# First expert layer of a two-layer decoder: expert tiles taken in pairs, the two 48-channel tails in different partition halves

## Chip, cores and metric

The program runs on one core of a Trainium2 chip. The metric is the device time of one execution in microseconds (us). Its engines are named as in the profile: PE is TensorE (PEld its weight loads, PEldq its instruction queue), DVE is VectorE, ACT is ScalarE, POOL is GpSimd, SP is SyncE, which here issues transfers (SPq).

## What is computed

A decoder of two layers over 32 sequences of 64 tokens, 256 channels, all in float32. Each layer has a self attention, a cross attention and a mixture of experts, each followed by a layer norm. The change lies in the first mixture of experts: 2048 tokens, 16 experts of 176 inner channels, the best 4 for each token, and a shared part.

```python
scores = jax.nn.softmax(xt @ Wg.T, axis=-1)
...
topi = jax.lax.top_k(masked, TOPK)[1]
weights = jnp.take_along_axis(scores, topi, axis=1) * ROUTE_SCALE
combine = jnp.zeros((T, E), xt.dtype).at[jnp.arange(T)[:, None], topi].add(weights)
h = jax.nn.silu(jnp.einsum('td,eid->eti', xt, W1)) * jnp.einsum('td,eid->eti', xt, W3)
expert_out = jnp.einsum('eti,edi->etd', h, W2)
y = jnp.einsum('etd,te->td', expert_out, combine)
z = jax.nn.silu(xt @ Ws1.T) * (xt @ Ws3.T) @ Ws2.T
```

## The kernel before

Everything stands in one program; the stages follow each other in blocks, and all engines meet at a barrier at the end of a block. The block `moe0` (from L1278) is the first mixture of experts. Tokens are copied by GpSimd into `xs`, a table in memory sorted by expert, of 79 tiles (`NT`) of 128 rows, each tile of one expert. Then each engine runs its own loop over the 79 tiles, four tiles to a turn of the loop (`tile_pipeline`, L1189), with the last seven written out; waits on semaphores couple the loops. For one tile the steps are:

- SyncE (`load`) reads the tile's place from a table and fetches its 128 rows of 256 channels into one of four buffers `XG`.
- TensorE (`rows`, L1590) turns them with two transposes; ScalarE (`rows`, L1455) copies them to `XGT`.
- TensorE (`gate_up`, L1598) multiplies with the expert's `W13`: 352 columns, 176 for the gate and 176 for up, over two halves of the 256 channels. A float32 product is two passes in the trace, so these are four instructions.
- ScalarE (`silu`, L1459) takes the silu of the gate, VectorE (`product`, L1534) multiplies it with up into `H` (128 tokens x 176 channels).
- TensorE (`turn_product`, L1604 and L1605) turns `H` in two pieces, 128 channels and the tail of 48; ScalarE copies both into `HT` (L1463, L1464). Rows 48 to 127 of the tail piece are zero, set once by GpSimd.
- TensorE multiplies with `W2A` (L1618, the first 128 inner channels) and `W2B` (L1620, the tail; its rows 48 to 127 are zeros, loaded by SyncE), 256 columns each.
- VectorE (`step`, L1542) copies the result to `Y`, ScalarE (`store`) issues its transfer to `ys`.

The register with the expert's number is loaded by `expert(j)` (L1585) before gate and up and again before W2A.

Two more things run beside it. GpSimd, when it has scattered the tokens, gathers the results of the first 12 token tiles (`EARLY`) from `ys`, four rows of results for each token, and adds them to `X` (`fetch_row` L1212, `add_rows`). After the tenth of these (`t == 9`) it computes a root for the next layer norm (`root_on_pool`, L1269 and L1270). VectorE leaves its loop twice for that norm: at tile 56 for the moments, at tile 68 for the normalization, which waits for the root:

```python
if t == 9:
    fx.l1.root_on_pool(nc, pool, fx.neghalf, own)
...
tile_pipeline(dve, step, NT, ((56, lambda: fx.l1.moments_on_dve(nc, dve, fx.X, r.steps)),
                              (68, lambda: fx.l1.apply_on_dve(nc, dve, fx.X))))
```

At the end TensorE has five filling products (`busy`, L132), and then comes the barrier.

## Time and profile before

| | us |
|---|---|
| median of three runs | 1228.31 |
| lowest and highest | 1223.89, 1232.03 |
| profiled execution, its time | 1227.53 |
| profiled execution, its span | 1225.5 |
| loop of the first experts on TensorE | 424.2 to 622.5 |
| barrier behind it | 627.2 |

The span runs from the first to the last instruction of the program; the time has 2.0 us more around it. In a line of the timeline the columns are the start, the duration, engine, line, operation, what is written and read, and how many instructions in a row; in square brackets is how long the engine was idle before and what ended it. The busy time of a product on PE contains its way through the array, so two products that follow each other without a gap overlap in the timeline: what one costs is the distance of two starts.

### The profile page before, as it was taken

To read this page: it belongs to the slowest core of one execution; us is meant where nothing else is said; L and a number is where in the kernel's file an instruction comes from. 1 tells how busy PE (TensorE), PEld (TensorE's weight loads), DVE (VectorE), ACT (ScalarE), POOL (GpSimd) and SP (SyncE) were. 2 spreads that over 40 slices of the span, in tenths; PEclk is the share of its full clock that TensorE was granted. 3 is DMA by queue.
4 is the path that set the end of the run, shared out by engine and by line. 5 is a ranking of instruction groups with operands and counts; after the bars stand their busy time and mean duration, and the time that the engine had idled before them with its cause. 6 is when DMAs were issued, how large, how long until landed. Compare 5 with 4: busy or idle time off the path is not lost. (4 is left out here: it accounts for less than half of the span.)

```text
span 1225.5 us, 29187 instructions
## 1 busy us (share of the span) xinstructions
PE 1107.1 (90%) x10342; PEld 871.7 (71%) x10343; DVE 474.1 (39%) x1234; ACT 500.3 (41%) x1301; POOL 443.6 (36%) x565
## 2 busy tenths in 40 slices
PE   5889888999989899999987999988649999999997
PEld 2567676776645577777766778776528989999997
DVE  1226465455557133323335666664383000000422
ACT  0424544344443233333335566664403434333342
POOL 2022012131124886787735664223034200200433
PEclk8999999999999999999989999999878999999999
DMA  6039918202137365565453110000056655655672
GB/s 196 18 93 356 352 36 301 96 24 75 53 138 231 121 197 176 159 195 148 136 215 154 42 50 19 20 20 2 5 177 224 206 168 175 205 172 173 202 242 83
DMA packets 116521, 173.18 MB, mean 141 GB/s; under 512 B 17440, under 2 KB 94096, under 8 KB 114960
## 3 DMA queue, kind: packets, MB, share of 16 engines
q1 hardware_dynamic: 89936, 128.46, 32.1%
q0 software_dynamic: 9696, 26.75, 6.7%
q10 hardware_dynamic: 16784, 16.49, 4.1%
q8 instruction: 76, 1.25, 0.4%
q14 instruction: 29, 0.24, 0.1%
HBM read 105.07 MB, written 65.27 MB: 139 GB/s over the span
## 5 line engine op out<-in xcount | busy, mean ns | idle before, releaser
L2589 PE MATMUL bank<-m_XGT,m_w 128*128 128x128 f32 x1248 | 149.4, 279 | 0.0
L2589 PEld LDWEIGHTS bank<-m_XGT,m_w 128*128 128x128 f32 x1248 | 146.4, 196 | 0.5 <-issue 0.5
L2603 PE MATMUL bank<-w,m_HT 128*128 x624 | 141.0, 379 | 0.0
L2603 PEld LDWEIGHTS bank<-w,m_HT 128*128 128x128 f32 x624 | 115.8, 190 | 14.0
L2421 ACT ACTIVATE m_HT<-bank,m_b 128x128 f32<-128x128 f32 x312 | 88.8, 368 | 81.9 <-PE bank L2589 78.5
L1598 PE MATMUL bank<-m_W,m_XGT 128*128 x316 | 107.1, 462 | 0.6 <-ACT m_XGT L1455 0.5
L2381 POOL DMA_INDIRECT m_GA<-ys,r_pos x32 | 32.1, 1005 | 130.0 <-SPq L2336 121.3
L1455 ACT ACTIVATE m_XGT<-bank 128x256 f32<-128x256 f32 x79 | 30.3, 383 | 119.8 <-DVE m_US L1542 117.6
L1212 POOL DMA_INDIRECT GA<-ys,r_pos x64 | 64.3, 1005 | 31.4 <-issue 22.7
L381 POOL TENSOR_SCALAR l_rs<-l_mv 128x2 f32<-128x2 f32 x16 | 3.6, 225 | 194.2 <-DVE l_mv L622 194.0
L1392 POOL DMA_INDIRECT xs<-X,r_pos x64 | 63.4, 990 | 27.1 <-issue 13.7
L1534 DVE TENSOR_TENSOR m_H<-bank,m_SG 128x176 f32<-128x176 f32 x79 | 27.0, 341 | 117.1 <-ACT m_SG L1459 117.1
L1598 PEld LDWEIGHTS bank<-m_W,m_XGT 128*128 128x128 f32 x316 | 54.0, 191 | 18.4 <-issue 1.5
L2367 POOL DMA_INDIRECT xs<-X,r_pos x32 | 32.0, 1000 | 61.1 <-DMA xs<-X,r_pos 35.2
L2432 ACT ACTIVATE m_Y<-bank 128x256 f32<-128x256 f32 x39 | 15.0, 383 | 92.4 <-PE bank L2603 92.4
L1618 PE MATMUL bank<-m_W2A,inputs 128*128 x158 | 47.6, 384 | 1.6 <-ACT inputs L1464 0.9
L1831 ACT ACTIVATE l_WX<-bank 128x512 f32<-128x512 f32 x64 | 33.8, 603 | 35.1 <-PE bank L2086 35.1
L1620 PE MATMUL bank<-m_W2B,inputs 128*128 x158 | 47.0, 379 | 0.0
L1542 DVE COPY m_US<-bank 128x256 f32<-128x256 f32 x79 | 33.5, 425 | 34.3 <-PE bank L1620 31.6
L59 PE MATMUL bank<-XT,inputs 128*128 128x512 f32 x96 | 43.1, 595 | 1.5 <-ACT raw L451 0.8
L2505 DVE TENSOR_TENSOR X<-bank,X 128x512 f32<-128x512 f32 x8 | 5.5, 692 | 89.8 <-PE bank L2565 89.8
L498 ACT ACTIVATE l_W<-l_W 128x512 f32<-128x512 f32 x32 | 19.4, 630 | 48.7 <-DVE l_W L648 48.7
(369 smaller groups left out, 2311.6 us busy)
## 6 DMA issues: line engine op xcount, KB each, us to landing
m_w<-in_m_w SPq DMA_DIRECT2D x35, 1024.0 KB, 5.2
xs<-zeros SPq DMA_DIRECT2D x1, 10112.0 KB, 33.7
ys<-zeros SPq DMA_DIRECT2D x1, 10112.0 KB, 36.0
ys<-m_US ACTq DMA_DIRECT2D x79, 128.0 KB
m_GS<-xs SPq DMA_DIRECT2D x72, 128.0 KB, 2.2
w<-in_m_w SPq DMA_DIRECT2D x8, 1024.0 KB, 14.9
m_W<-in_w SPq DMA_DIRECT2D x2, 2816.0 KB, 13.6
xs<-zeros SPq DMA_DIRECT2D x1, 4992.0 KB, 19.1
```

The source lines that it names most:

```text
L59: last = nc.tensor.matmul(dst, stills[i], movings[i], start=i == 0, stop=i == n - 1)
L1212: pool.indirect_dma_start(out=fx.GA[:, t % 2 * (t < EARLY), k, :], out_offset=None, in_=fx.ys, in_offset=bass.IndirectOffsetOnAxis(ap=fx.p ...
L1392: pool.indirect_dma_start(out=fx.xs, out_offset=bass.IndirectOffsetOnAxis(ap=r.pos[:, t, k:k + 1], axis=0), in_=fx.X[:, t, :], in_offset=N ...
L1542: nc.vector.tensor_copy(Y[:, b % 2, :], BY[b % 2][:, 0:DIM]).then_inc(y_used, 1)
L1598: last = nc.tensor.matmul(BU[b % 2][:, 0:IW], XGT[:, b % 2, m * P:(m + 1) * P], W13[:, m, bass.ds(e, 1), :], start=m == 0, stop=m == KC - 1)
L1618: nc.tensor.matmul(BY[b % 2][:, 0:DIM], HT[:, b % 2, 0, :], W2A[:, bass.ds(e, 1), :], start=True, stop=False)
L1620: nc.tensor.matmul(BY[b % 2][:, 0:DIM], HT[:, b % 2, 1, :], W2B[:, bass.ds(e, 1), :], start=False, stop=True).then_inc(y_full, 1)
L1831: nc.scalar.activation(WX[:, t, r].rearrange("p m c q -> p (m c q)"), SB[r][:], ACT.Exp, scale=D32 ** -0.5).then_inc(x_used.sem, 1)
L2381: pool.indirect_dma_start(out=GA[:, t, k, :], out_offset=None, in_=fx.ys1, in_offset=bass.IndirectOffsetOnAxis(ap=fx.pos1[:, t, k:k + 1], ...
L2421: last = nc.scalar.activation(HT[:, b % 2, at, :], BU[i][:, c * P:(c + 1) * P], ACT.Gelu, bias=b1[:, b % WB, at:at + 1])
L2589: last = nc.tensor.matmul(BU[i][:, c * P:(c + 1) * P], w1[:, b, m, lo:lo + P], XGT[:, b % 2, m * P:(m + 1) * P], start=m == 0, stop=m == K ...
L2603: last = nc.tensor.matmul(BY[b % 2][:, 0:DIM], HT[:, b % 2, c, :], w2[:, bass.ds(e, 1), c, :], start=c == 0, stop=c == CH - 1)
```

## The change

The loops take two tiles at a time (`pair_pipeline`). For a pair j, j+1:

- VectorE writes the first 128 channels of each product to its own buffer of `H`, and the two tails of 48 side by side into a third, at columns 0 and 64. Three transposes in place of four turn them; the tails then lie in partitions 0 to 47 and 64 to 111 of one piece. ScalarE copies all three with one instruction.
- The tail of tile j is multiplied with `W2B` over 48 rows. The tail of tile j+1 needs its weights in partitions 64 to 111, so SyncE loads them for each pair into a small buffer `odd` (48 x 256), two buffers in turn, and TensorE waits for `ld_odd`. The zeros of `W2B` are no longer loaded, and GpSimd clears a quarter of what it cleared.
- TensorE keeps the expert's number in a register from gate and up to W2A where both lie in the same turn of the loop: six loads for four tiles in place of eight.
- The order of the steps changes on each engine. TensorE goes gate and up of both next tiles, rows of the two after, W2A twice, the tails, and the turn of the next pair.

```diff
+def pair_pipeline(engine, step, n, visits=(), done=0):
+
+    for at, visit in (*visits, (n - PEEL, None)):
+        with engine.Fori(done // 4, at // 4) as i:
+            for b in range(0, 4, 2):
+                step(i * 4 + b, b, None)
+        if visit:
+            visit()
+        done = at
+    for j in range(n - PEEL, n, 2):
+        step(j, j % 4, n - 1 - j)
...
-        W2A, W2B = sb("W2A", [P, E0, DIM]), sb("W2B", [P, E0, DIM])
+        W2A, W2B, odd = sb("W2A", [P, E0, DIM]), sb("W2B", [P, E0, DIM]), sb("odd", [P, 2, DIM])
-        SG, H, HT = sb("SG", [P, 2, I0]), sb("H", [P, 2, I0]), fx.HT
+        SG, H, HT = sb("SG", [P, 2, I0]), sb("H", [P, 3, P]), fx.HT
...
-                sp.dma_start(W2B[KI:P], fx.zeros[KI:P].unsqueeze(1).broadcast_to([P - KI, E0, DIM])).then_inc(ld_w, 16)
                 sp.wait_ge(r.placed, 2)
 
+                def load_odd(e, b):
+                    sp.dma_start(odd[HALF:HALF + KI, b // 2].unsqueeze(1),
+                                 io["w2"][P:I0, bass.ds(e, 1), :]).then_inc(ld_odd[b // 2], 16)
+
+                def expert(j):
+                    return sp.value_load(r.texp[0:1, bass.ds(j, 1)], min_val=0, max_val=E0 - 1)
+
                 def load(j, b, checked=None):
+                    if b % 2:
+                        e = expert(j - BEHIND)
                     if checked is not None:
                         need = sp.value_load(r.tneed[0:1, bass.ds(checked, 1)], min_val=1, max_val=TILES)
                     s = sp.value_load(r.tslot[0:1, bass.ds(j, 1)], min_val=0, max_val=NT - 1)
                     sp.wait_ge(t_full, j + 1)
+                    if b % 2:
+                        load_odd(e, (b - BEHIND) % 4)
...
+                for j in range(NT - BEHIND, NT - 1, 2):
+                    e = expert(j)
+                    sp.wait_ge(y_full, j - 3)
+                    load_odd(e, j % 4)
...
-                def turned_product(j, b):
-                    act.wait_ge(ht_full, j + 1)
-                    nc.scalar.activation(HT[:, b % 2, 0, :], BH[b % 2][:, 0:P], ACT.Copy)
-                    nc.scalar.activation(HT[0:KI, b % 2, 1, :], BH[b % 2][0:KI, P:2 * P], ACT.Copy).then_inc(ht_used, 1)
+                def turned_pair(j):
+                    act.wait_ge(ht_full, j + 2)
+                    nc.scalar.activation(HT[:, 0:3, :].rearrange("p c t -> p (c t)"), BH[0][:, 0:3 * P],
+                                         ACT.Copy).then_inc(ht_used, 2)
 
                 def store(j, b):
                     s = act.value_load(r.tslot[0:1, bass.ds(j, 1)], min_val=0, max_val=NT - 1)
@@ -1469,13 +1497,18 @@
                     act.dma_start(rows_out[:, bass.ds(s, 1), :], Y[:, b % 2, :].unsqueeze(1)).then_inc(stored[b % 2], 16)
 
                 def step(j, b, ahead):
-                    if follows(ahead, 3):
-                        rows(j + 3, b + 3)
                     if follows(ahead, 2):
                         silu(j + 2, b + 2)
-                    if follows(ahead, 1):
-                        turned_product(j + 1, b + 1)
-                    store(j, b)
+                    if follows(ahead, 3):
+                        silu(j + 3, b + 3)
+                    for k in (4, 5):
+                        if follows(ahead, k):
+                            rows(j + k, b + k)
+                    if follows(ahead, 2):
+                        turned_pair(j + 2)
+                    for k in range(2):
+                        if follows(ahead, k):
+                            store(j + k, b + k)
...
                 silu(0, 0)
                 shared_rows(PAIRS - 1)
+                silu(1, 1)
                 rows(2, 2)
                 load(6, 2)
-                silu(1, 1)
-                turned_product(0, 0)
-                tile_pipeline(act, step, NT)
+                rows(3, 3)
+                turned_pair(0)
+                pair_pipeline(act, step, NT)
...
                 def product(j, b):
                     dve.wait_ge(gate, j + 1)
-                    nc.vector.tensor_tensor(H[:, b % 2, :], BU[b % 2][:, I0:IW], SG[:, b % 2, :],
+                    at = HALF * (b % 2)
+                    nc.vector.tensor_tensor(H[:, b % 2, :], BU[b % 2][:, I0:I0 + P], SG[:, b % 2, 0:P], ALU.mult)
+                    nc.vector.tensor_tensor(H[:, 2, at:at + KI], BU[b % 2][:, I0 + P:IW], SG[:, b % 2, P:I0],
                                             ALU.mult).then_inc(h_done, 1)
 
-                def step(j, b, ahead):
-                    if follows(ahead, 2):
-                        product(j + 2, b + 2)
+                def result(j, b):
                     dve.wait_ge(y_full, j + 1)
                     dve.wait_ge(stored[b % 2], 8 * (j + (2 - b % 2)))
                     nc.vector.tensor_copy(Y[:, b % 2, :], BY[b % 2][:, 0:DIM]).then_inc(y_used, 1)
 
+                def step(j, b, ahead):
+                    for k in (2, 3):
+                        if follows(ahead, k):
+                            product(j + k, b + k)
+                    for k in range(2):
+                        if follows(ahead, k):
+                            result(j + k, b + k)
+
+                dve.wait_ge(padded, 2)
                 product(0, 0)
                 product(1, 1)
-                tile_pipeline(dve, step, NT, ((56, lambda: fx.l1.moments_on_dve(nc, dve, fx.X, r.steps)),
+                pair_pipeline(dve, step, NT, ((56, lambda: fx.l1.moments_on_dve(nc, dve, fx.X, r.steps)),
                                               (68, lambda: fx.l1.apply_on_dve(nc, dve, fx.X))))
...
                 def gate_up(j, b):
-                    e = expert(j)
+                    e = kept[b % 4] = expert(j)
                     pe.wait_ge(t_used, j + 1)
                     for m in range(KC):
                         last = nc.tensor.matmul(BU[b % 2][:, 0:IW], XGT[:, b % 2, m * P:(m + 1) * P],
                                                 W13[:, m, bass.ds(e, 1), :], start=m == 0, stop=m == KC - 1)
                     last.then_inc(u_full, 1)
 
-                def turn_product(j, b):
-                    pe.wait_ge(h_done, j + 1)
-                    nc.tensor.transpose(BH[b % 2][:, 0:P], H[:, b % 2, 0:P], fx.ident[:])
-                    nc.tensor.transpose(BH[b % 2][0:KI, P:2 * P], H[:, b % 2, P:I0], fx.ident[:]).then_inc(ht_full, 1)
-
-                def step(j, b, ahead):
+                def turn_pair(j, ahead):
+                    pe.wait_ge(h_done, j + (2 if follows(ahead, 3) else 1))
+                    nc.tensor.transpose(BH[0][:, 0:P], H[:, 0, :], fx.ident[:])
                     if follows(ahead, 3):
-                        rows(j + 3, (b + 3) % 4)
+                        nc.tensor.transpose(BH[0][:, P:2 * P], H[:, 1, :], fx.ident[:])
+                    nc.tensor.transpose(BH[0][:, 2 * P:3 * P], H[:, 2, :], fx.ident[:]).then_inc(ht_full, 2)
+
+                def down_pair(j, b, both, first, e):
+                    if not first:
+                        pe.wait_ge(y_used, j)
+                    pe.wait_ge(ht_used, j + 2)
+                    if both:
+                        pe.wait_ge(ld_odd[b // 2], 4 * (j - b) + 16)
+                    for k in range(len(e)):
+                        nc.tensor.matmul(BY[k][:, 0:DIM], HT[:, k, :], W2A[:, bass.ds(e[k], 1), :],
+                                         start=True, stop=False)
+                    nc.tensor.matmul(BY[0][:, 0:DIM], HT[0:KI, 2, :], W2B[0:KI, bass.ds(e[0], 1), :],
+                                     start=False, stop=True).then_inc(y_full, 1)
+                    if both:
+                        nc.tensor.matmul(BY[1][:, 0:DIM], HT[HALF:HALF + KI, 2, :], odd[HALF:HALF + KI, b // 2, :],
+                                         start=False, stop=True).then_inc(y_full, 1)
+
+                kept = [None] * 4
+
+                def step(j, b, ahead, first=False):
+                    e = [kept[b], kept[b + 1]] if b % 4 == 2 else [None, None]
+                    for k in (2, 3):
+                        if follows(ahead, k):
+                            gate_up(j + k, b + k)
+                    both = follows(ahead, 1)
+                    for k in range(2):
+                        if e[k] is None and (k == 0 or both):
+                            e[k] = expert(j + k)
+                        if follows(ahead, k + 4):
+                            rows(j + k + 4, (b + k) % 4)
+                    down_pair(j, b, both, first, e[0:2 if both else 1])
                     if follows(ahead, 2):
-                        gate_up(j + 2, b + 2)
-                    if follows(ahead, 1):
-                        turn_product(j + 1, b + 1)
-                    e = expert(j)
-                    if not follows(ahead, 2):
-                        pe.wait_ge(y_used, j - 1)
-                    pe.wait_ge(ht_used, j + 1)
-                    nc.tensor.matmul(BY[b % 2][:, 0:DIM], HT[:, b % 2, 0, :], W2A[:, bass.ds(e, 1), :],
-                                     start=True, stop=False)
-                    nc.tensor.matmul(BY[b % 2][:, 0:DIM], HT[:, b % 2, 1, :], W2B[:, bass.ds(e, 1), :],
-                                     start=False, stop=True).then_inc(y_full, 1)
+                        turn_pair(j + 2, ahead)
 
                 pe.wait_ge(sh_used, 2 * SC * GROUPS)
                 rows(0, 0)
                 rows(1, 1)
                 shared_down(GROUPS - 1, (0,))
                 pe.wait_ge(r.placed, 3)
-                pe.wait_ge(ld_w, 80)
+                pe.wait_ge(ld_w, 64)
                 gate_up(0, 0)
                 shared_down(GROUPS - 1, (1,))
+                gate_up(1, 1)
                 rows(2, 2)
-                gate_up(1, 1)
-                turn_product(0, 0)
+                rows(3, 3)
+                turn_pair(0, None)
                 pe.wait_ge(z_used, PAIRS)
-                tile_pipeline(pe, step, NT)
+                step(0, 0, None, True)
+                step(2, 2, None)
+                pair_pipeline(pe, step, NT, done=4)
```

On TensorE, inside the loop, for one tile before. L1590 are rows, L1598 gate and up, L1604 and L1605 the turn, L1618 W2A, L1620 W2B:

```order
L1590 MATMUL bank<-ident,m_GS 128x128 x2
L1585 ISA
L1585 TENSOR_LOAD r_table
L1585 ISA x2
L1596 REGISTER_ALU
L1598 ISA
L1598 MATMUL bank<-m_W,m_XGT 128x352
L1598 ISA
L1598 MATMUL bank<-m_W,m_XGT 128x352
L1604 MATMUL bank<-ident,m_H 128x128
L1605 MATMUL bank<-ident,m_H 48x128
```

and the second half of a pair's steps in the changed kernel, the same engine and place, without register loads between (L1641 gate and up, L1633 rows, L1659 W2A, L1661 and L1664 the tails, L1647 to L1650 the turn):

```order
L1641 MATMUL bank<-m_W,m_XGT 128x352
L1641 ISA
L1641 MATMUL bank<-m_W,m_XGT 128x352
L1633 MATMUL bank<-ident,m_GS 128x128 x4
L1659 ISA
L1659 MATMUL bank<-m_W2A,inputs 128x256
L1659 ISA
L1659 MATMUL bank<-m_W2A,inputs 128x256
L1661 REGISTER_ALU
L1661 MATMUL bank<-m_W2B,inputs 128x256
L1664 MATMUL bank<-m_odd,inputs 128x256
L1647 MATMUL bank<-ident,m_H 128x128
```

The turn stood directly behind the next tile's gate and up, one tile behind its own; now it stands behind the tails and follows its own pair's gate and up by rows, W2A and tails.

On VectorE, at the end of the loop that leads to tile 68, before:

```order
L1534 TENSOR_TENSOR m_H<-bank,m_SG 128x176
L1542 COPY m_US<-bank 128x256
L1192 REGISTER_ALU
L1192 COMPARE_AND_BRANCH
L1275 TENSOR_SCALAR X<-X,l_mv,l_rs 128x256 x4
```

and in the changed kernel:

```order
L1569 TENSOR_TENSOR m_H<-bank,m_SG 128x128
L1570 TENSOR_TENSOR m_H<-bank,m_SG 128x48
L1575 REGISTER_ALU
L1576 COPY m_US<-bank 128x256 x2
L1205 REGISTER_ALU
L1205 COMPARE_AND_BRANCH
L1288 TENSOR_SCALAR X<-X,l_mv,l_rs 128x256 x4
```

The products and the copies now come in twos; the normalization (four instructions behind the wait for the root) stands where it stood, after the copy of tile 67.

## Rows read from the trace of the kernel before

**Rows 1.** The page's table of engines: busy us, share of the span.

```profile
PE 1107.1 (90%) x10342; PEld 871.7 (71%) x10343; DVE 474.1 (39%) x1234; ACT 500.3 (41%) x1301; POOL 443.6 (36%) x565
```

**Rows 2.** Timeline of TensorE, one tile of the first experts and the next.

```profile
500.77 0.38 PE L1590 MATMUL bank<-ident,m_GS 128*128 128x128 f32 x2
500.99 1.35 PE L1598 MATMUL bank<-m_W,m_XGT 128*128 x4
502.18 0.27 PE L1604 MATMUL bank<-ident,m_H 128*128 128x128 f32 x1
502.29 0.27 PE L1605 MATMUL bank<-ident,m_H 128*48 128x128 f32 x1
502.40 0.60 PE L1618 MATMUL bank<-m_W2A,inputs 128*128 x2
502.83 0.60 PE L1620 MATMUL bank<-m_W2B,inputs 128*128 x2
503.26 0.38 PE L1590 MATMUL bank<-ident,m_GS 128*128 128x128 f32 x2
```

**Rows 3.** Timeline of all engines around VectorE's visit at tile 68.

```profile
596.41 0.42 DVE L1542 COPY m_US<-bank 128x256 f32<-128x256 f32 x1 [0.39 <-PE bank L1620]
...
597.63 1.04 POOL L1270 TENSOR_TENSOR l_rs<-l_rs,neghalf 128x4 f32<-128x4 f32 x1
...
598.71 1.38 DVE L1275 TENSOR_SCALAR X<-X,l_mv,l_rs 128x256 f32<-128x256 f32 x4 [1.87 <-POOL l_rs L1270]
...
600.39 0.33 PE L1604 MATMUL bank<-ident,m_H 128*128 128x128 f32 x1
```

**Rows 4.** Timeline of GpSimd, the first fetch of two neighbouring token tiles.

```profile
576.60 1.03 POOL L1212 DMA_INDIRECT GA<-ys,r_pos  x1 [1.37 <-issue]
...
587.59 1.03 POOL L1212 DMA_INDIRECT GA<-ys,r_pos  x1 [1.37 <-DVE m_US L1542]
```

**Rows 5.** Timeline of the end of the block, all engines.

```profile
615.43 0.72 POOL L1232 TENSOR_TENSOR X<-X,GA 128x256 f32<-128x256 f32 x1
...
622.07 0.59 PE L1620 MATMUL bank<-m_W2B,inputs 128*128 x2
...
622.50 4.46 PE L132 MATMUL bank<-ones 128*128 128x512 f32 x10
...
627.22 1.91 POOL L1765 MEMSET l_VS<- 128x2176 f32 x1 [11.07 <-POOLq L1318]
```

**Rows 6.** Timelines of TensorE and its weight loads around column halves.

```profile
167.41 0.63 PE L810 MATMUL bank<-ident,X 128*128 128x128 f32 x4 [0.39 <-DVE l_V L579]
167.97 2.12 PE L855 MATMUL bank<-l_V,l_W 128*64 128x68 f32 x64
170.01 0.70 PE L59 MATMUL bank<-inputs,l_xwk 128*128 128x512 f32 x1
...
170.55 0.19 PEld L59 LDWEIGHTS bank<-inputs,l_xwk 128*128 128x128 f32 x1 [0.24 <-issue]
170.98 0.19 PEld L59 LDWEIGHTS bank<-inputs,l_xwk 128*128 128x128 f32 x1 [0.24 <-issue]
```

**Rows 7.** Timeline of TensorE at the loop's start.

```profile
424.19 0.38 PE L1590 MATMUL bank<-ident,m_GS 128*128 128x128 f32 x2
```

**Rows 8.** Timeline from gate and up to the product, ScalarE and VectorE.

```profile
504.88 0.31 ACT L1459 ACTIVATE m_SG<-bank 128x176 f32<-128x176 f32 x1
...
505.22 0.34 DVE L1534 TENSOR_TENSOR m_H<-bank,m_SG 128x176 f32<-128x176 f32 x1 [1.24 <-ACT m_SG L1459]
```

**Rows 9.** Line L1585, 500 to 600 us: ns min, median, max of the loads.

```profile
L1585 PEldq TENSOR_LOAD <-r_table x78: 295/302/628, 500.6 to 597.5; - x78
```

**Rows 10.** Waits of SyncE, 500 to 630 us: total, times, longest.

```profile
SPq L1338 <- PE bank L1590: 45.7, 37, 2.5
```

**Rows 11.** The page's DMA issues: KB each, median us to landing.

```profile
m_W2B<-zeros SPq DMA_DIRECT2D x1, 1280.0 KB, 33.2
```

**Rows 12.** Windows of 4 us: busy per engine, then PEclk, DMA share, GB/s.

```profile
630.00:634.00 4.00, 2.81 (x8) 2.25 (x8) 0.00 (x0) 1.15 (x2) 2.10 (x5) 0.50 0.98 337
```

10 lines of the change are left out of this document (5 added, 5 removed).

## The prediction, made before the changed kernel ran

> **What bounds the kernel now.** The page's table of engines comes first: TensorE is busy 90% of the span, no other engine over 41% [rows 1]. That is an average over six stages, so the next view is the stretch that the change touches: the timeline of the first expert layer. One tile there is six steps on TensorE, and their starts are the whole period: the two transposes of rows take 0.22 us (500.77 to 500.99), gate and up 1.19, the two transposes of H 0.11 each, W2A 0.43, W2B 0.43, and the next tile starts at 503.26, 2.49 after this one [rows 2]. No step waits. So a tile costs what TensorE issues, and two tiles 4.98 us.
>
> But the layer ends where three engines meet, and there a second view matters: who waits for whom at the visit that VectorE makes at tile 68 (apply_on_dve). Its copy of tile 67 starts at 596.41, then it sits idle for 1.87 us until GpSimd's power instruction (start 597.63, in root_on_pool) is done, and starts the four normalizations at 598.71; TensorE's next transpose of H is at 600.39, some 0.3 us late [rows 3]. GpSimd is not waiting for the experts at that time: it fetches and adds one token tile per 10.99 us (576.60, 587.59, with gaps for which the profile names its own issue or the usual 1.37 us) [rows 4]. The root hangs behind the tenth of these. So **the tenth token tile on GpSimd, at 598.7 us, is a fixed date**, and TensorE now arrives at it almost exactly on time. After it come tiles 68 to 78 on TensorE; the last W2B starts at 622.07, the five filling matmuls at 622.50, and all engines pass the barrier at 627.2 [rows 5].
>
> **The change part by part, on TensorE, per two tiles.** Removed: one of four transposes of H, 0.11 us. Kept: four row transposes (0.44), two times gate and up (2.38), three transposes (0.33), two W2A (0.86), together 4.01 us, from [rows 2]. What is left is the price of the two tails, 0.86 us today as two W2B products over 128 rows. They now use 48 rows each, one from partition 0 and one from partition 64, so they are matmuls of the 64-row form. Fewer rows shorten nothing by themselves: a start-to-start step goes with the columns that stream (0.22 for 256 per pass, 0.11 for 128). What could shorten is the pair running side by side. The trace has no two row halves with 128 columns, but it has column halves: 64 passes of 68 columns take 2.04 us (167.97 to 170.01) [rows 6]. A pass of 128 columns steps by 0.11, so 64 of 68 columns one after another would be some 3.7; two at a time did run. The bounds for the tails are then 0.43 us (fully side by side), 0.64 (each product has two passes, and if they are issued product by product only the middle two overlap) and 0.86 (no overlap). I take 0.43, which the column halves are nearest to.
>
> The same rows price what is added: entering and leaving that form. Four transposes starting at 167.41 should occupy 4 x 0.11 plus a cold first step of 0.03; the next form starts after 0.56, so 0.09 is lost. In the 2.04 us, 32 steps of 68/128 x 0.107 make 1.82, so 0.22 is lost inside and at the exit, of which I put half on the exit. The first full-width pass then takes 0.54 us to the second (170.01 to 170.55), where later ones step by 0.43 (170.55 to 170.98): another 0.11, because its weights were not loaded ahead [rows 6]. Entering costs the same exposed weight load, some 0.1. Together 0.09 + 0.1 + 0.09 + 0.1 = **0.38 us for each visit**, one visit per pair; ends 0.25 and 0.55. The pair is then 4.01 + 0.43 + 0.38 = 4.82 us against 4.98: 0.16 saved per pair, 6 us over 39.5 pairs, if nothing else held the layer.
>
> What the row shows is a loss at each boundary. The Trainium skill says the same in "TensorEngine Tiling (Array Packing)", Tiling Modes, Key Properties: changing the tiling mode drains TensorE. It speaks against this change, and the trace agrees with it. The same page's Theoretical Speedup table offers up to twice the rate for a dimension of 64 or less; taken alone that would make the pair 4.44 us and 21 us in all, and the boundary losses above take 15 of them away.
>
> **The latency of the pair.** The turn of H now waits for the product of a tile whose gate and up ended only 0.44 + 0.86 + 0.43 + 0.2 = 1.9 us before. The chain is: silu starts 0.2 us after the last gate pass has been followed (504.67, a pitch after 502.18, to 504.88), lasts 0.31, the product starts at 505.22 and lasts 0.34 [rows 8]; split in two instructions it is some 0.47. That is 1.1 us, under 1.9, so the wait is covered by rows, W2A and tails; were that cover gone it would cost 0.2 to 1.1 us per pair. Queued behind this wait on TensorE is the next gate and up with its register load.
>
> **Registers.** A load of an expert number takes TensorE's sequencer 0.30 us [rows 9] and stands beside running matmuls now, since [rows 2] has no gap. Two of eight per four tiles go. Value: 0. **ScalarE** makes one copy of 384 columns instead of two copies: off the path, 0. **SyncE**: one more register load and one more 48 KB transfer per pair. It now waits 45.7 us for TensorE in 37 loads from 500 on, 1.24 us of 2.49 [rows 10], so a load costs it 1.25 and the pair 2.5 plus some 1.25 for the new one, 3.75 of 4.82: still ahead. The new transfer is asked for after the rows of tile j+5 and needed 5.7 us later; at the one place where SyncE issues the next layer's weights it may come up to 4 us late, once, before tile 68. **W2B's zeros** (1,280 KB, landed 33.2 us after issue at 358) [rows 11] are gone, but their cover was 25 us: 0. In the **start**, the loop begins with rows at 424.19 [rows 7]; gate and up of tile 1 now stands directly before its own turn, so some 1 us is lost there.
>
> **The sum.** Result of tile 67: 425.2 + 34 x 4.82 = 589.1, plus the 3.1 us of small stalls that lie between 424.19 and 596.41 today (172.2 us for 68 x 2.486 = 169.1): 592.2. VectorE then waits 6 us for the root at 598.7, not 1.9. Nothing of what was won before that date is left. TensorE can still do the next 4.8 us of work (to 597) and then stands idle until the products of tiles 70 and 71 are there: 598.7 + 1.3 for the normalizations + 0.9 for four product instructions, so 601.0. From there: turn 0.33, pairs 70 and 72 9.64, pair 74 with one set of rows 4.60, pair 76 with one gate and up 1.19 + 0.86 + 0.81 + 0.22 = 3.08, and the last single tile with an exposed copy 1.8. End at 620.4, against 622.5. An idle stretch has its price too: after 2.4 us idle at 627 the granted clock of 630 to 634 is 0.50, the 1.2 GHz level [rows 12]. Half a clock for 3.4 us costs 1.7 us of work, so 622.1 (bounds 620.4 and 623.9). Against 622.5 that is -0.4 us, between -2 and +1.4. GpSimd's own end moves by under 1 us from 616.2 and stays before it [rows 5], the filling matmuls and everything later are unchanged. The profiled execution took 1227.5 us; minus 0.4 is 1227.1, and the median of the three runs stands 0.8 above, so **1228 us**. A difference of 1%, 12.3 us, is about what a measurement of this kernel tells from none.
>
> **Rivals.** (a) *The tails do not overlap* and still pay the boundaries: 4.01 + 0.86 + 0.38 = 5.25 us per pair, 0.27 more than today. Tile 67 comes after 606, so the date no longer matters (1.1 us back), the start costs 1: 39 x 0.27 = 10.5, 1239 us. This is the case on the slow side; it decides once the pair is over some 5.0 us. For it: the two passes of a product must follow each other, and no row shows two row halves. Against: the column halves. The half-way case (0.64) gives 5.03 per pair, +2 to +3, 1231 us. (b) *GpSimd's date moves with TensorE*, that is, its ten tiles wait for expert results after all. Then the gain of 6 us is kept, some 5 net of the start: 1223 us, or with no boundary cost 15 more, 1208. Against it: in [rows 4] each fetch starts the same 10.99 us after the last. (c) *The boundaries cost nothing in a loop like this*: 4.44 per pair. Tile 67 would be done by 579, TensorE idle 17 us, the rest takes 17.6 us plus up to 3.4 for the clock: 619 to 622, so 1225 to 1228. This shows how little the pair's length decides. The page's speedup rule named above would, without the date, be the upper gain in (b); with the date it is this case.
>
> **Chances.** Forecast and case (c) together 0.70, half-way case 0.10, (a) 0.13, of which nearly half is over 1%, (b) 0.04, something unforeseen on the slow side 0.03. That gives faster by over 1%: 0.04, within 1%: 0.86, slower by over 1%: 0.10. The range reaches from 1223 (the lower bound of (c) and the spread of the runs shown, 1223.9 to 1232.0) to 1239, which takes in (a).
>
> **What would show it.** VectorE's idle time before the normalizations at tile 68 grows from 1.9 to some 6 us (17 or more in case (c), none in (a)), with the normalizations still at 598 to 599. The rows transposes of neighbouring pairs stand 4.8 us apart; between the last W2A pass and the first tail pass, and again before the turn, a tenth of a microsecond is missing each time. TensorE is idle for some 4 us before 601, and the granted clock falls after it. The barrier stays near 627. I would be wrong if the normalizations come much earlier than 598, or if the pair is over 5.3 us because a wait on the odd buffer, on the product or on a store ends last in it.

## The result, and the profile after

The changed kernel took **1241.09 us** (median of 4 runs, 1239.0 to 1242.85) against 1227.21 of the kernel before (4 runs): ratio 1.0117, 95% interval 1.0088 to 1.0147. It is slower, by 13.9 us where -0.4 was forecast. The profiled execution took 1239.0 us, its span is 1236.9. In two of the four comparisons below every kernel, the one before too (1277 and 1284 us), took 4 to 5% longer, for a reason that stays open, and the traces taken there show the first four to six pairs at 5.6 to 17.6 us each; those runs are read by their ratio and by their later pairs.

The page of the changed kernel first, its table of engines, which answers to [rows 1]:

```profile
PE 1105.9 (89%) x10303; PEld 846.6 (68%) x10304; DVE 473.1 (38%) x1313; ACT 491.2 (40%) x1183; POOL 443.9 (36%) x565
```

TensorE has 1.2 us less to do in a span 11.4 us longer. So it is idle time that came. The timeline of TensorE, two pairs, answers to [rows 2]:

```profile
503.98 0.33 PE L1647 MATMUL bank<-ident,m_H 128*128 128x128 f32 x1
...
504.36 2.53 PE L1641 MATMUL bank<-m_W,m_XGT 128*128 x8
506.73 0.60 PE L1633 MATMUL bank<-ident,m_GS 128*128 128x128 f32 x4
507.17 1.03 PE L1659 MATMUL bank<-m_W2A,inputs 128*128 x4
508.13 0.48 PE L1661 MATMUL bank<-m_W2B,inputs 48*128 x1
508.13 0.48 PE L1664 MATMUL bank<-m_odd,inputs 48*128 48x256 f32 x1
...
508.76 0.33 PE L1647 MATMUL bank<-ident,m_H 128*128 128x128 f32 x1
...
509.58 2.63 PE L1641 MATMUL bank<-m_W,m_XGT 128*128 x8 [0.27 <-issue]
512.04 0.38 PE L1633 MATMUL bank<-ident,m_GS 128*128 128x128 f32 x2
512.91 0.43 PE L1633 MATMUL bank<-ident,m_GS 128*128 128x128 f32 x2 [0.48 <-issue]
513.23 1.13 PE L1659 MATMUL bank<-m_W2A,inputs 128*128 x4
514.28 0.48 PE L1661 MATMUL bank<-m_W2B,inputs 48*128 x1
```

The pair from 503.98 to 508.76 is 4.78 us, without a gap, and its two tails start together (508.13): that is the pair of the prediction. The next one, behind the loop's turn, has two gaps for which the profile names no releaser but issue. From W2A to W2A it is 513.23 - 507.17 = 6.06. All through the loop the two lengths alternate: 4.88 and 5.0 to 6.22 us, seventeen long ones, together 18.9 us above 4.88.

What issue stands for is seen in TensorE's sequencer (PEldq). Its instructions in the long pair, by source line: the loop's branch (L1205), the loads of expert numbers (L1628), and the wait ahead of W2A (L1657). Columns: count, duration in ns (min/median/max), first and last start.

```profile
L1205 PEldq COMPARE_BRANCH  x1: 208/208/208, 508.3 to 508.3; - x1
...
L1628 PEldq TENSOR_LOAD <-r_table x4: 301/384/568, 508.7 to 512.0; - x4
...
L1657 PEldq FUSED_REGOPS  x1: 47/47/47, 513.0 to 513.0; - x1
```

The product of this pair is ready at 508.15; only then does the sequencer get past its wait for it. Behind it come the branch and four loads, 1.10 us apart (508.7 to 512.0 in three steps), and W2A can be issued at 513.1. That is 4.9 us in the queue (508.15 to 513.1). The array has less to do in that time: 0.38 for the turn, 2.38 for gate and up and 0.44 for rows from 508.76 on, so it could have started W2A at 511.96. It started 1.27 us later.

The odd tail's load is late once, at the weights' visit of SyncE:

```profile
541.91 1.12 PE L1659 MATMUL bank<-m_W2A,inputs 128*128 x4 [2.02 <-DMA m_odd<-in_w]
```

The visit at tile 68, which answers to [rows 3]:

```profile
597.75 1.04 POOL L1283 TENSOR_TENSOR l_rs<-l_rs,neghalf 128x4 f32<-128x4 f32 x1
...
608.32 0.76 DVE L1576 COPY m_US<-bank 128x256 f32<-128x256 f32 x2 [0.81 <-PE bank L1664]
608.99 1.38 DVE L1288 TENSOR_SCALAR X<-X,l_mv,l_rs 128x256 f32<-128x256 f32 x4
...
615.60 1.10 POOL L1225 DMA_INDIRECT GA<-ys,r_pos  x1 [16.81 <-DVE m_US L1576]
```

GpSimd's root comes at 597.8 to 598.8 as before. But the result of tile 67 comes at 608.3, 12 us later than before, so VectorE does not wait for the root: the date that was to swallow a gain stands ten microseconds before the tiles, and it swallows nothing of a loss. The one who waits is GpSimd, 16.8 us for its next fetch; its last addition ends at 630.3 and not at 616.2, still ahead of TensorE. The end, which answers to [rows 5]:

```profile
634.68 0.69 PE L1659 MATMUL bank<-m_W2A,inputs 128*128 x2 [2.10 <-DVE m_US L1576]
...
635.93 4.56 PE L132 MATMUL bank<-ones 128*128 128x512 f32 x10
```

The filling matmuls start at 635.93 against 622.50, 13.4 us later, and the barrier is passed at 640.75 and not at 627.2. (The span is only 11.4 us longer; the 2 us between, behind the barrier, were not followed.) From the first W2A pass (427.27 before, 425.69 after) it is 195.2 us before and 210.2 after: 15.0 more. Worked out: long pairs +18.9, the odd load +2.2 (7.07 for 4.88), 36 pairs of 4.88 for 4.98 at -3.6, the old small stalls at tiles 44 and 68 at -2.2, makes 15.3.

### The profile page after: what moved, and what is told of

Its sections match the earlier page's. It is cut to its first block and busy times, and to the rows that moved or that the text cites. A ratio compares the mean times of both kernels' runs of the same rounds, so it can differ in the third digit from the quotient of the medians.

```text
span 1236.9 us, 29227 instructions
## 1 busy us (share of the span) xinstructions
PE 1105.9 (89%) x10303; PEld 846.6 (68%) x10304; DVE 473.1 (38%) x1313; ACT 491.2 (40%) x1183; POOL 443.9 (36%) x565
## 5 line engine op out<-in xcount | busy, mean ns | idle before, releaser
L1641 PE MATMUL bank<-m_W,m_XGT 128*128 x316 | 102.0, 465 | 5.2 <-issue 5.2
L1641 PEld LDWEIGHTS bank<-m_W,m_XGT 128*128 128x128 f32 x316 | 56.7, 190 | 34.3 <-issue 12.7
L1569 DVE TENSOR_TENSOR m_H<-bank,m_SG 128x128 f32<-128x128 f32 x79 | 22.7, 287 | 114.8 <-ACT m_SG L1487 114.7
L1487 ACT ACTIVATE m_SG<-bank 128x176 f32<-128x176 f32 x79 | 21.9, 316 | 80.3 <-PE bank L1641 68.1
L1576 DVE COPY m_US<-bank 128x256 f32<-128x256 f32 x79 | 30.4, 420 | 55.9 <-PE bank L1664 51.7
L1659 PE MATMUL bank<-m_W2A,inputs 128*128 x158 | 42.7, 392 | 4.2 <-DVE m_US L1576 2.1
L1491 ACT ACTIVATE inputs<-bank 128x384 f32<-128x384 f32 x40 | 19.6, 490 | 59.7 <-PE bank L1650 59.7
```

Source lines behind the costliest of these rows:

```text
L1576: nc.vector.tensor_copy(Y[:, b % 2, :], BY[b % 2][:, 0:DIM]).then_inc(y_used, 1)
L1641: last = nc.tensor.matmul(BU[b % 2][:, 0:IW], XGT[:, b % 2, m * P:(m + 1) * P], W13[:, m, bass.ds(e, 1), :], start=m == 0, stop=m == KC - 1)
L1659: nc.tensor.matmul(BY[k][:, 0:DIM], HT[:, k, :], W2A[:, bass.ds(e[k], 1), :], start=True, stop=False)
```

## The experiments

**1. One load more in the kernel before** (label before_plus). Here the theory is that loads on the sequencer had little room left even before.

```
 def step(j, b, ahead):
...
     e = expert(j)
+    if ahead is None:
+        expert(j)
     if not follows(ahead, 2):
         pe.wait_ge(y_used, j - 1)
```

> The kernel before, with one more load of the expert's number per tile on TensorE (three, not two) whose value nobody uses. Theory S (a load is 1.0 to 1.1 us of the sequencer, of which the tile of 2.49 us has room for two and hardly more): the tile becomes 3.2 to 3.5 us and the time 1280 to 1300. Rival, as in my prediction (a load of 0.30 us stands beside running matmuls): 2.49 us and no change.

Measured in one run: 1255.68 us, 29.6 more than the 1226.09 of the kernel before. Four tiles take 11.9 us where they took 9.96, in tiles of about 2.8, 2.65, 2.7 and 3.7 us. Two rows of its timeline at the loop's turn:

```profile
528.99 1.45 PE L1598 MATMUL bank<-m_W,m_XGT 128*128 x4 [0.28 <-issue]
...
531.15 0.69 PE L1620 MATMUL bank<-m_W2A,inputs 128*128 x2 [0.49 <-ACT inputs L1464]
```

The expectation was too high, its rival of no cost is out. In the changed kernel a load with its address and range instructions takes 0.75 us, from 509.72 to the start of what follows at 510.47, and its matmuls' own register work brings the pitch to 1.10. Four more of 0.75 are 3.0 us and cost 1.94, so the kernel before had about 1.1 us of room in four tiles of 9.96 (an estimate from these two numbers). A load was hidden, but not free.

**2. Expert numbers carried over the loop's turn** (carried), so that the long pair has two loads instead of four behind its wait.

```
 def gate_up(j, b):
     e = kept[b % 4] = expert(j)
+    if b % 4 < 2:
+        pe.reg_mov(held[b % 4], e)
...
-    e = [kept[b], kept[b + 1]] if b % 4 == 2 else [None, None]
+    e = [kept[b], kept[b + 1]] if b % 4 == 2 else [pe.snap(held[k], min_val=0, max_val=E0 - 1) for k in range(2)]
```

> The changed kernel, with the expert numbers carried in two registers over the turn of the loop, so that TensorE loads four numbers for four tiles and not six. Theory S (TensorE's sequencer: the pair behind the loop's turn has four register loads in a row, about 1.1 us each with what belongs to them, while the array has only some 3 us of issued work): the long pairs of 6.0 us fall to 4.9 to 5.2, tile 67 is done some 17 us earlier, VectorE then waits 5 to 7 us for GpSimd's root at 598 to 599, and the time is 1226 to 1230, level with the kernel before. Theory T (the long pair waits for SyncE's rows, or for the loop's branch): it stays at 6.0 us and the time at 1240.

Measured: 1234.28 us, ratio 1.0065 (1.0041 to 1.0089). Nearly half of the loss is back, less than expected: the long pair is 5.44 us, not 4.9 to 5.2, and the short one 4.78. What is left of the long pair's excess lies between the turn and gate, where the branch and the first load still stand behind the wait:

```profile
502.83 0.27 PE L1652 MATMUL bank<-ident,m_H 128*128 128x128 f32 x1
503.51 2.63 PE L1643 MATMUL bank<-m_W,m_XGT 128*128 x8 [0.41 <-issue]
```

The turn's last step is 0.11, so gate could start at 502.94; it starts 0.57 later. A second cost is plainer here than in the changed kernel. SyncE's queue and TensorE at the weights' visit:

```profile
524.66 0.39 SPq L1267 DMA_DIRECT2D l_wq<-in_sa_wq  x1
...
527.94 0.47 SPq L1268 DMA_DIRECT2D l_rw<-in_rw  x1
...
531.45 0.35 SPq L1345 DMA_DIRECT2D m_odd<-in_w  x1
...
535.01 1.22 PE L1661 MATMUL bank<-m_W2A,inputs 128*128 x2 [3.22 <-DMA m_odd<-in_w]
```

```profile
532.00:536.00 4.00, 0.99 (x2) 0.84 (x3) 0.61 (x4) 0.63 (x3) 3.45 (x5) 0.75 0.74 232
536.00:540.00 4.00, 4.00 (x12) 2.21 (x11) 0.75 (x2) 0.49 (x1) 2.68 (x4) 0.50 0.28 78
```

The seven weight loads hold the queue from 524.66 to 528.4, the odd load goes out at 531.45, 7.9 us behind the one before it where 4.9 is usual, and lands some 3.5 us later where 1.8 is usual; the array waits 3.22 us for it. So the queue makes it late by 3 us and the landing by 1.7. In the windows the number behind POOL is the granted clock: 0.75 with the wait in it, then 0.50, the 1.2 GHz level. The two pairs take 8.16 and 7.65 for 4.78 and 5.44: 5.6 us, 3.2 of them for the wait; the rest, 2.4, is put down to the clock.

**3. The visit at tile 68 moved behind the last tile** (carried_late), and **4. both tails over 128 rows** (full_rows). full_rows contains the edit of carried_late; in it the odd tail uses W2B rows 0 to 47 with zeros below, so it leaves out the odd tile's tail channels; the time is that of two ordinary products.

```
-    pair_pipeline(dve, step, NT, ((56, lambda: fx.l1.moments_on_dve(nc, dve, fx.X, r.steps)),
-                                  (68, lambda: fx.l1.apply_on_dve(nc, dve, fx.X))))
+    pair_pipeline(dve, step, NT, ((56, lambda: fx.l1.moments_on_dve(nc, dve, fx.X, r.steps)),))
+    fx.l1.apply_on_dve(nc, dve, fx.X)
...
-    nc.tensor.matmul(BY[0][:, 0:DIM], HT[0:KI, 2, :], W2B[0:KI, bass.ds(e[0], 1), :],
+    nc.tensor.matmul(BY[0][:, 0:DIM], HT[:, 2, :], W2B[:, bass.ds(e[0], 1), :],
-        nc.tensor.matmul(BY[1][:, 0:DIM], HT[HALF:HALF + KI, 2, :], odd[HALF:HALF + KI, b // 2, :],
+        nc.tensor.matmul(BY[1][:, 0:DIM], HT[:, 2, :], W2B[:, bass.ds(e[1], 1), :],
```

> As the run with carried registers, and the normalization that waits for GpSimd's root is moved from tile 68 behind the last tile on VectorE. If the date of the root binds (theory D), the experts end 3 to 6 us earlier than with carried registers alone: filling matmuls at 617 to 619, time 1222 to 1225. If the wait on VectorE costs TensorE nothing: equal to that run, within 1 us in the trace.

> As carried_late, but both tails are multiplied over all 128 rows, as in the kernel before (W2B's zeros loaded again; the odd tile's tail is multiplied with the wrong rows, so its 48 channels are left out of the result and only the time counts). Theory B (two tails side by side take half the time and lose it again in entering and leaving the 64-row form): the pair is 4.01 + 0.86 = 4.87 us, equal to the 4.88 of the changed kernel within 0.1, and the time equal to carried_late within 4 us. Rival (the form is worth its full 0.43 us a pair, the rest of the pair being dearer than I think): the pair is 5.3 us and the time 1238 or more.

Measured: 1234.39 (ratio 1.0059, 1.0033 to 1.0085) and 1232.98 (1.0060, 1.0032 to 1.0088). The first expectation missed: with pairs this slow the tiles come after the root (root at 592.8 to 593.8, tile 67 at 600.7 in the carried kernel), so moving the visit gives nothing. The second is met. TensorE's timelines of the tails, first side by side (carried), then one after another (full_rows):

```profile
500.96 1.03 PE L1661 MATMUL bank<-m_W2A,inputs 128*128 x4
501.92 0.48 PE L1663 MATMUL bank<-m_W2B,inputs 48*128 x1
...
502.24 0.38 PE L1663 MATMUL bank<-m_W2B,inputs 48*128 x1
...
502.56 0.33 PE L1649 MATMUL bank<-ident,m_H 128*128 128x128 f32 x1
502.72 0.27 PE L1651 MATMUL bank<-ident,m_H 128*128 128x128 f32 x1
```

```profile
498.04 1.03 PE L1662 MATMUL bank<-m_W2A,inputs 128*128 x4
498.90 0.59 PE L1664 MATMUL bank<-m_W2B,inputs 128*128 x2
499.33 0.59 PE L1667 MATMUL bank<-m_W2B,inputs 128*128 x2
499.77 0.27 PE L1650 MATMUL bank<-ident,m_H 128*128 128x128 f32 x1
```

Side by side: entering costs 0.10 (0.96 for 0.86), the tails 0.64, leaving 0.05 (0.16 for 0.11), 0.79 in all. One after another: 0.87. The short pairs are 4.78 and 4.86. So the side-by-side form gives 0.08 us per pair, 3 us in the layer, which these medians don't resolve.

**5. The turn at the head of the next step** (turn_first, and again as turn_again): the branch now comes ahead of the wait.

```
 def step(j, b, ahead, first=False):
     e = [kept[b], kept[b + 1]] if b % 4 == 2 else [None, None]
+    if not first:
+        turn_pair(j, ahead)
     for k in (2, 3):
         if follows(ahead, k):
             gate_up(j + k, b + k)
...
-    if follows(ahead, 2):
-        turn_pair(j + 2, ahead)
```

> The changed kernel with one thing moved: the turn of a pair's product, with its wait for the product, stands at the head of the next step instead of at the end of its own, so that the loop's branch comes ahead of that wait, under the down matmuls. TensorE's instructions keep their order; the four register loads of the step (two for gate and up, two for down) stay behind the wait. In the changed kernel the pairs alternate between 4.88 us and about 6.05 us. If what stands behind the wait on TensorE's queue makes the long pair (branch 0.4 us and loads of about 1 us each with their checks), the long pair falls by the branch, about 0.4 us to 5.6, seventeen times, and the time by 7 to 1234 us. Rival: the long pair comes from the product's own latency (1.4 us from the gate's end to the product); then it stays near 6.05 and the time at 1241.

> The changed kernel with the turn at the head of the next step and nothing else, as in the earlier run of this edit, whose chip took 1277 us for the kernel before. In that trace the long pair was 5.25 us and the short one 4.88. Against a kernel before of 1227 us: 17 x (6.05 - 5.25) = 13.6 us less than the changed kernel's 1241 would be 1228; the ratio there was 1.005, which would be 1233. Between them: 1229 to 1234.

Measured: ratios 1.0050 (1.0018 to 1.0081) and 1.0072 (1.0037 to 1.0106). Past the disturbed first pairs the long pair is 5.25 us, the short one 4.88, in both: 0.8 less than in the changed kernel, where the branch alone was reckoned at 0.4. A long pair of turn_first on TensorE, and the four loads in its queue:

```profile
516.33 1.03 PE L1659 MATMUL bank<-m_W2A,inputs 128*128 x4
...
521.59 0.91 PE L1659 MATMUL bank<-m_W2A,inputs 128*128 x3
```

```profile
L1628 PEldq TENSOR_LOAD <-r_table x4: 297/300/312, 517.5 to 520.6; - x4
```

With all four loads still behind the wait, the pair lost two thirds of its excess. Most of the other 0.4 us stands in the loads themselves: in the changed kernel's long pair the third and the fourth last up to 568 ns, here all four are at 297 to 312. Over all turns from 500 to 600 us the third and fourth loads last 441 and 536 ns on average in the changed kernel, 299 and 327 with the turn first, 0.35 us less together. Why a load gets longer is not shown. The rival, that the product's latency makes the whole excess, is out: that chain was not touched. The expected 1229 to 1234 us can't be read from a comparison at 1284. As ratios they are 1.001 to 1.006; 1.0050 lies in that, 1.0072 above it, with an interval that reaches into it.

**6. Turn at the head, carried numbers, and the next loads ahead of the wait** (rotated), and **7. SyncE's weight loads in four groups** (rot_split).

```
+    ours = [expert(j + k) if follows(ahead, k) else None for k in (2, 3)]
+    if not first:
+        turn_pair(j, ahead)
...
-    for upto, visit in ((48, weights), (NT - (NT - done) % 4, None)):
+    for upto, visit in ((44, weights(0, 2)), (48, weights(2, 4)), (52, weights(4, 5)), (56, weights(5, 7)), (NT - (NT - done) % 4, None)):
```

> The kernel with carried expert numbers, its turn moved to the head of the step as above, and the two register loads of the next gate matmuls taken ahead of the wait too, so that only address arithmetic stands between the wait and the gate matmuls. There the pairs alternate between 4.78 and 5.44 us. If the sequencer's work behind the wait is all of the excess of 0.66, both pairs come to 4.8 us, 17 x 0.66 = 11 us are saved and the time is 1223 us. Rival: the product's latency or the instruction fetch at the branch holds the array, the long pair stays over 5.2 us and the time at 1230 or above. The stall at the weights' visit (5.6 us over two pairs) stays in either.

> The rotated kernel with SyncE's seven weight loads of the next layer in four small groups (2, 2, 1, 2) between four turns of its loop instead of in one at tile 48. In the kernel with carried numbers the odd tail's load, issued behind all seven (528.0 to 531.45 us), landed at 535.0 and the array waited 3.2 us for it and then ran two pairs partly at half the clock: 8.16 and 7.65 us in place of 4.78 and 5.44, 5.6 us in all. If SyncE's queue is the cause, these two pairs come to 4.8 to 5.5 us and the time is about 5 us below the rotated kernel, 1218 us. Rival: the transfers themselves, not their issue, hold the odd load up (16 engines full with the weights); then the stall is only spread over four places and the time stays within 1 us of the rotated kernel.

Measured: ratios 1.0013 (0.9981 to 1.0045) and 0.9995 (0.9967 to 1.0022). Both expectations missed: as ratios to a kernel before of 1227 us they were 0.997 and 0.993. The rotated kernel's long pair is 4.9 to 5.6, not 4.8. The profile of rot_split says why. The sequencer's loads and, of TensorE, the turn:

```profile
L1629 PEldq TENSOR_LOAD <-r_table x2: 301/441/581, 511.8 to 512.9; - x2
```

```profile
512.44 0.38 PE L1664 MATMUL bank<-m_W2B,inputs 48*128 x1
...
513.62 0.33 PE L1650 MATMUL bank<-ident,m_H 128*128 128x128 f32 x1 [0.79 <-issue]
```

The loads now stand between the tails' issue and the turn, with the branch 2.4 us of queue against 1.7 us of work. The load work was moved from one thin place to another. The split does what it should: the two pairs at the visit are 4.78 and 5.55 instead of 8.94 and 7.73. (It thins out the queue and the transfers alike, so it does not tell the one's part from the other's.) A further kernel, rot_split with the visit at tile 68 last (rot_split_late), was expected 12 us ahead of the kernel before and came out level with it, at 0.9999 (0.9966 to 1.0031).

> The kernel with spread weight loads and VectorE's normalizations (the visit at tile 68) behind its last tile. If both former causes are gone, tile 67's result is taken near 590 us, ahead of the root that GpSimd gives at about 598; in the kernel with spread loads VectorE then waits some 8 us at the visit and TensorE half of that. Behind the last tile nothing queues up behind that wait: 3 to 4 us less, 1214 us, which would be 12 us faster than the kernel before. Rival: the date of the root sets the end in any order (the next layer needs it), then it equals the kernel with spread loads.

**8. Every load where the array is fed** (hoisted; with the weights split, hoist_split).

```
+    if b % 4 == 0:
+        kept[:] = [pe.snap(h, min_val=0, max_val=E0 - 1) for h in held]
+    own, following = kept[0:2], kept[2:4]
...
+    if not first:
+        turn_pair(j, ahead)
+    for k in range(2):
+        if follows(ahead, k + 2):
+            gate_up(j + k + 2, b + k + 2, following[k])
+    loaded = [expert(j + k + 4) if follows(ahead, k + 4) else None for k in range(2)]
...
+    down_pair(j, b, both, first, own[0:2 if both else 1])
+    kept[:] = following + loaded
+    if b % 4 == 2:
+        for h, e in zip(held, kept):
+            if e is not None:
+                pe.reg_mov(h, e)
```

> The turn at the head of the step, and every register load of TensorE taken where the array is fed: a pair's two expert numbers are loaded once, right behind the eight gate and up matmuls (2.5 us of issued work) of the pair before, and carried in four registers over the loop's turn for the gate and for the down matmuls. In the rotated kernel the sequencer still took two loads and the branch between the down matmuls (issued 511.09) and the turn (issued 513.52), 2.4 us against 1.7 us of array work, a gap of 0.8 us before the turn. If the sequencer's work near the wait is the whole excess, both pairs come to 4.8 us: 36 x (4.98 - 4.8) = 6 us less than the kernel before and, with the 5.6 us stall at the weights' visit left, about level with it, 1226 us on a chip where the kernel before takes 1227 (ratio 1.00). Rival: the product's latency (1.3 us behind the gate's end) holds the long pair over 5.1 us; then the ratio stays at 1.003 or above.

> The same with the seven weight loads in four groups of 2, 2, 1, 2 at four turns of SyncE's loop. If SyncE's queue makes the stall (5.6 us with carried numbers), it goes and the ratio to the kernel before is about 0.995 to 0.996. Rival: the transfers themselves make it; then the ratio equals the hoisted kernel's.

> The same with VectorE's normalizations behind its last tile. With all pairs at 4.8 us tile 67's result comes near 592 us and the root near 598; if that date holds the tiles up, this kernel is 2 to 4 us below the one with spread loads, ratio 0.992 to 0.993. Rival: the next layer waits for the same root, then the two are equal.

Measured: hoisted 0.9999 (0.9964 to 1.0035), hoist_split 0.9951 (0.9917 to 0.9986), hoist_split_late 0.9960 (0.9926 to 0.9994). Nearly every pair is now 4.78 us; of hoisted all but those at the start, two at 508 to 520 us with an odd load 1.3 us late, and the visit (8.91 and 6.50, which the split takes away). hoist_split_late was expected 2 to 4 us ahead of hoist_split and is not: in these slower executions the root comes late too, at 622.1 in hoist_split, and the visit costs TensorE only 1.0 us (a pair of 5.77):

```profile
623.21 1.38 DVE L1289 TENSOR_SCALAR X<-X,l_mv,l_rs 128x256 f32<-128x256 f32 x4 [2.76 <-POOL l_rs L1284]
```

**9. Undisturbed** (after_split, hoist_split_2, hoist_split_late_2): the changed kernel with split weights alone, and the last two again.

> The changed kernel with SyncE's seven weight loads in four groups (2, 2, 1, 2) and nothing else. In its trace the two pairs at that visit took 7.07 and 5.00 us against 4.88 and 6.05 before and behind them: 1.1 us. If SyncE's queue made that, this is 1 us faster than the changed kernel (1240), too little to measure, and the trace shows no wait of TensorE on the odd tail's load. Rival: the load waits for the transfers, and the wait is spread over four places.

> The kernel with hoisted loads and spread weight loads again, since in its first comparison the kernel before took 1284 us and the first five pairs 8 to 17 us each. In that trace every later pair took 4.78 us. Where those first pairs run at 4.8 us too, tile 77's result comes 36 x 0.20 = 7 us earlier than in the kernel before: ratio 0.995, 1220 us. Rival: a date behind the tiles (the root near 598 us) then holds the end: ratio 0.998 to 1.

> The same with VectorE's normalizations behind its last tile, again. If the root's date (597.8 us in the changed kernel, 598.7 in the kernel before) holds the tiles up once they are early, this is 2 to 4 us faster than the kernel with spread loads: ratio 0.992. Rival: equal to it.

Measured: after_split 1244.97 us, ratio 1.0125 (1.0073 to 1.0177); its pair at the visit is 4.88, its long pairs 5.65 to 6.42. The odd load was 1 to 2 us of the changed kernel's loss, below what a run tells. hoist_split_2: 1227.28, ratio 0.9999 (0.9975 to 1.0024). Its pairs are 4.78 us on either side of the loop's turn:

```profile
501.74 1.03 PE L1662 MATMUL bank<-m_W2A,inputs 128*128 x4
...
506.52 1.03 PE L1662 MATMUL bank<-m_W2A,inputs 128*128 x4
```

Its timeline around the visit at tile 68:

```profile
587.04 0.42 DVE L1577 COPY m_US<-bank 128x256 f32<-128x256 f32 x1 [0.83 <-DMA ys<-m_US]
...
591.21 1.04 POOL L1284 TENSOR_TENSOR l_rs<-l_rs,neghalf 128x4 f32<-128x4 f32 x1
592.29 1.38 DVE L1289 TENSOR_SCALAR X<-X,l_mv,l_rs 128x256 f32<-128x256 f32 x4 [4.82 <-POOL l_rs L1284]
...
594.36 0.33 PE L1650 MATMUL bank<-ident,m_H 128*128 128x128 f32 x1 [3.90 <-DVE m_H L1571]
```

```profile
594.00:598.00 4.00, 3.65 (x10) 2.30 (x11) 1.16 (x5) 0.81 (x2) 2.28 (x3) 0.63 0.22 68
```

VectorE waits 4.82 us for the root, TensorE 3.90 for products, the granted clock of the next window is 0.63, and the pair takes 10.45 us. That is the prediction's own picture of the visit, 5.7 us of loss. The whole gain is not in it: in the trace the layer is still 3.8 us shorter from first to last W2A pass than in the kernel before (190.5 for 194.3), which the medians don't show. With the visit last (hoist_split_late_2) no one waits:

```profile
592.48 0.76 DVE L1577 COPY m_US<-bank 128x256 f32<-128x256 f32 x2 [0.81 <-PE bank L1667]
...
598.06 1.04 POOL L1284 TENSOR_TENSOR l_rs<-l_rs,neghalf 128x4 f32<-128x4 f32 x1
```

1222.70 us, ratio 0.9968 (0.9943 to 0.9992): 4 us faster than the kernel before (1 to 7 by the interval), some 18 faster than the changed kernel. First to last W2A pass it takes 185.4 us, the kernel before 194.3, the changed kernel 209.0. So the layer won 8.9 us in the trace and the medians show 4; where the rest goes was not followed.

## Why the prediction was wrong

**The step that failed** is "Registers ... Value: 0", with the sentence ahead of it, that what is queued behind the wait on TensorE is the next gate and up with its register load. The queue was named and not priced. A load was taken at the 0.30 us of its row [rows 9] and as lying beside running matmuls because [rows 2] has no gap. Both are wrong readings. The distance of two loads in the trace of before was to be had from the same view, some 1.0 us within a tile:

```profile
L1585 PEldq TENSOR_LOAD <-r_table x2: 300/306/312, 500.6 to 501.7; - x2
```

In the long pair it is 1.10. The Trainium skill says in "Perfetto Trace Analysis", Sequencer-only Instruction, that the profiler reports an instruction's execution alone, without fetch, wait and semaphore push. The trace agrees: the four instructions of one load report 0.52 us together, 0.30 of it the load, and take 0.75 from the first one's start to the start of what follows. And a load lies beside matmuls only while the queue is ahead of the array. A wait that is released late takes the lead away: it is released 0.6 us before the array needs the turn, and then 4.9 us of queue stand against 3.8 us of array work. Experiments 2, 5 and 8 take this apart: the long pair of some 6.05 us is 5.44 with fewer loads behind the wait, 5.25 with the branch ahead of it, and 4.78 with the loads under gate and up. The product's chain is the same in all of them.

**What bounds the kernel.** "No step waits, so a tile costs what TensorE issues" was right for the array and hid a second resource, the queue, with about 1.1 us of room in ten (experiment 1).

**The pair of 4.82 us** was right: 4.78 measured once nothing holds it. Its terms were not: tails 0.64 where 0.43 was taken, boundaries 0.15 where 0.38 was taken, two errors that cancel (0.79 and 0.81), so the right sum was luck. (By its own rows the boundaries were 0.09 + 0.1 + 0.11 + 0.11 = 0.41, not 0.38; that is 1 us in the layer.) The bound of 0.64, two passes of a product following each other, was the true one.

**Latency.** The chain was 1.1 us on paper. From the second gate's last pass (its end at about 506.9) to the last product's end (508.15) it is 1.3, and the turn starts at 508.76, so it is covered, as forecast.

**SyncE.** "Up to 4 us late, once, before tile 68" was right in size and place: 2.0 us of wait in the changed kernel, 3.2 in the carried one. That it would be absorbed was not; and in the carried kernel another 2.4 us, put down to the clock, came behind the gap.

**The fixed date** was a true mechanism, shown by hoist_split_2 (4.8 us idle for 6 forecast, TensorE 3.9 for 4), but it only decides for a kernel whose tiles are early. In this one tile 67 came 16 us later than the 592.2 of the sum. Nor is it quite fixed. Counted from the first W2A pass to the start of the root's power instruction it is 167 us in hoist_split_2 and hoist_split_late_2, 170.4 in the kernel before, 172.1 in the changed one and 185.6 in before_plus: where tiles are slow, GpSimd waits for their results, 5.8 us at 510 in the changed kernel and 9.7 at 515 in before_plus, where 1.37 is usual.

**Rivals.** The slow rival (a), tails that don't overlap, gave nearly the right time (1239) for a reason that is not there: luck. Rival (b), a date that moves with TensorE, is small here: with the tiles 12 us late the root came at 597.8. It shows only in before_plus, where the root starts at 607.3. The closing sentence had the right threshold (over 5.3 us per pair; the mean is 5.5) and named waits on the odd buffer, on the product or on a store; what stood behind the wait on the product was missing from it. What came was the something unforeseen, which had a chance of 0.03; slower by over 1% had 0.10 in all.

## What to carry to other kernels

Price a register load by the distance between neighbouring loads on the sequencer, not by its own duration, and add up the queue between two late waits against the array's work in the same stretch: a kernel without gaps can be within a tenth of that limit. Put loads behind the longest issued block of matmuls, keep branches and loads from standing behind a wait that is released late, and don't queue a transfer that is needed soon behind a group that is not. A date set by another engine swallows gains only for those who reach it early; work out which side you are on before you count on it.

## What the runs showed of the hardware

Two 48-row products in different row halves start within 0.01 us of each other; their passes over 256 columns follow 0.32 us apart, where an ordinary pass takes 0.22. So two at once take 0.64 us for 0.86, not half. A branch at the loop's turn moved from behind a late wait to ahead of it gave 0.8 us: about 0.4 for the branch, and about 0.35 because the third and fourth loads behind it no longer last 441 and 536 ns but 299 and 327 on average. The same load took 0.30 us mostly in the kernel before; why some are longer was not tried. Behind a 3.2 us wait of the array the granted clock of 4 us windows was 0.75 and 0.50 (carried), behind one of 2.0 us it stayed at 1.00 (540 to 552 us of the changed kernel).
